# Eight heads of one attention item turned by VectorE and a DMA round trip instead of by TensorE

## Chip, cores and metric

One core of one Trainium2 chip runs the whole kernel. The metric is device microseconds of one execution; the kernel before took 1079.42 us (median of three runs: 1077.27, 1079.42, 1080.25).

## The reference, cut to what matters

All tensors are float32. There are 16 sequences of 128 tokens, width 512, 16 heads of 32 columns. The reference is a transformer layer followed by a second cross attention:

```
x  = x + attention(LN1(x) Wqkv) Wao            # stage A, mask_1x1xSxS2
x  = x + attention(LN2(x) Wq, ctx Wkv) Wco     # stage B, mask_Bx1xSxS2
x  = x + gelu(LN3(x) W1) W2                    # the MLP
x  = x + tanh(gate) * attention(x Wq', LNa(ctx) Wk', LNa(ctx) Wv') Wo'   # stage D, mask_BxS2
```

with, for each sequence and head,

```
P[q, k] = exp(scores[q, k] - max_k)      # scores = q k^T / sqrt(32), masked
out[q]  = (sum_k P[q, k] v[k]) / sum_k P[q, k]
```

TensorE contracts over the partitions. Softmax leaves the queries on the partitions of P, and the product with v needs the keys there, so each P (128 x 128, per head) has to be turned before the product.

## The kernel before

The attention stages are a software pipeline over 48 items: item g is sequence g % 16 of stage A (0 to 15), B (16 to 31) or D (32 to 47). Every engine has its own program, written out by hand in one order, and semaphores tie them together; there is no planner. `step` of each engine handles, in step g, the scores and softmax of item g, the turning and row sums of item g - 1, and the product with v, the context and the output projection of items g - 1 and g - 2 (`times_v(g - 2)`, `context(g - 2)`, `project_out(g - 2)`). Steps 46 and 47 of stage D stand in `last_steps_of_d`. Every projection is done as three products of split (hi, lo) parts.

A step also issues half units of the projections for the next pair of sequences on TensorE (L889, L897). Stage D has few of them left in its last steps: step 45 projects `units` 4 and 5 of the last pair.

There are three ways in which P is turned:

- By TensorE (`BY_PE`, L160): `exps` (L1397) writes the 16 heads to `prob`; `transpose_prob` (L919) turns them in four quarters of four heads (L935), two quarters at a time in banks 4 and 5 of PSUM; ScalarE copies quarters 0 and 2 back (`prob_out`, L1394), VectorE quarters 1 and 3 (L1850).
- Half and half (items neither in `BY_PE` nor in `WHOLE`): `exps` writes heads 0 to 7 to `prob_blocks` in an order of 32 x 32 blocks. VectorE transposes all the blocks in one instruction (`turn_blocks`, L1838 to L1841). Sync (the queue SP) stores the 512 KB to DRAM (`store_blocks`, L619 to L624), waits for the landing, and brings them back in four DMAs of 128 KB, each to 32 partitions of `prob` (`bring_blocks`, L626 to L633). TensorE turns only quarters 2 and 3, and ScalarE copies both in one instruction (`probs_out`, L1389; for item 43 as two of half the size, L1386).
- Whole (`WHOLE`, items 33 to 42): the second eight heads go the same way through `second_prob_blocks`.

`times_v(g)` (L968 to L994) waits for the copies and, for an exchanged item, for the four DMAs (`s_moved`, L979). The number of exchanges so far, the number of transposed quarters and of copies are derived from `BY_PE` by `moved_number`, `transposed_count`, `copied_by_act` and `copied_by_dve` (L167 to L194), so all waits follow the tuple.

The row sums of item g - 1 take their own way: `inverse_sums` on VectorE (L1835), a small transpose on TensorE (`row_sums`, L956), a copy by ScalarE (L1425), a store of 8 KB to DRAM (`store_row_sums`, L675) and four broadcast loads of 64 KB into `context` (`spread_row_sums`, L683), for which VectorE's `context` (L1856) waits.

Sync issues all DMAs in one order. In step 44 the last is (for an exchanged item) `store_blocks(44)`; in step 45 follow the mask of item 46, `store_stream(42)`, `bring_blocks(44)`, `store_row_sums(44)`, `spread_row_sums(44)`. Items 33 to 42 are whole, item 43 is half and half, items 44 to 47 are turned by TensorE. Step 45 has a special order on TensorE, since `sums_late(44)` (L450) is true: `times_v(43)`, `scores(45)`, both half units, `row_sums(44)`, two quarters of item 44, `project_out(43)` part 0, the other two quarters, part 1. The next instruction is `times_v(44)` (L1216).

Of the kernel before, what the change touches and what calls it, by code (L numbers as in the profile page):

```python
# [156 lines left out]

BY_PE = (0, 27, 28, 29, 30, 31, 44, 45, 46, 47)  # L160


WHOLE = tuple(range(33, 43))
# [3 lines left out]
def moved_number(g):  # L167

    return g + 1 - sum(k <= g for k in BY_PE)

# [6 lines left out]
def turned_by_pe(k):  # L177

    return 4 if k in BY_PE else 0 if k in WHOLE else 2


def transposed_count(g, c):

    return sum(turned_by_pe(k) for k in range(g)) + (c + 1 if g in BY_PE else c - 1)


def copied_by_act(g, half):

    return sum(turned_by_pe(k) // 2 for k in range(g)) + (half + 1 if g in BY_PE else 1)


def copied_by_dve(g, half):

    return sum(2 for k in range(g) if k in BY_PE) + (half + 1 if g in BY_PE else 0)  # L194

# [78 lines left out]
def build(nc, x, first_x, enc, encT, mask_a, mask_b, mask_d, weights, columns, rows, gate, ident_in, out):  # L274
# [3 lines left out]
    with ExitStack() as ctx:  # L278
# [160 lines left out]
        def item(st):  # L439

            return 16 * st.phase + st.b
# [4 lines left out]
        def value_bank(g, half):  # L446

            return T_BANK if g in WHOLE or g == 32 else T_BANK + half
# [62 lines left out]
        def sp_program():  # L511
# [114 lines left out]
            def bring_blocks(g):  # L626

                n = moved_number(g)
                sp.wait_ge(s_pst, 16 * n)
                blocks = turned[n % 2].rearrange("(i k) (j n) -> j k i n", i=4, j=4)  # L630
                for j in range(4):
                    dst = prob[32 * j:32 * j + 32, g % 2, 0:NH // 2 * T].rearrange("p (i n) -> p i n", i=4)
                    sp.dma_start(dst, blocks[j]).then_inc(s_moved, 16)  # L633

            def store_second_blocks(g):
                n = second_number(g)
                sp.wait_ge(s_turned2, n)
                if n > 2:
                    sp.wait_ge(s_moved2, 64 * (n - 2))
                sp.dma_start(turned_second[n % 2], second_blocks[:, :]).then_inc(s_pst2, 16)  # L640
# [67 lines left out]
            def step(st):  # L708
# [7 lines left out]
                if g - 1 in WHOLE:  # L716
                    store_second_blocks(g - 1)
                if st.prev and g - 1 not in BY_PE:
                    bring_blocks(g - 1)
# [1001 lines left out]
        def dve_program():  # L1721
# [67 lines left out]
            def make_mask_bias(g):  # L1789
                phase, b, par = g // 16, g % 16, g % 2  # L1790
                if phase == B:
                    dve.wait_ge(s_mask[par], 16 * (b // 2 + 1))
                    if b:
                        dve.wait_ge(s_biased, 2 * (g - 2) + 2 if b >= 2 else 32)
                    dve.tensor_scalar(mbias[:, par, :], msk[:, par, :], 1.0, 10000.0, ALU.subtract, ALU.mult).then_inc(s_mb, 1)
                if phase == D:
                    dve.wait_ge(s_mask[par], 16 * (8 + b // 2 + 1))
                    if b >= 2:
                        dve.wait_ge(s_masked, 2 * (g - 2) + 2)
                    dve.tensor_scalar(mbias[:, par, :], mrow[:, par, :], 1.0, 3e38, ALU.subtract, ALU.mult).then_inc(s_mb, 1)  # L1800
                    dve.wait_ge(s_mb, 16 + b + 1)
                    dve.tensor_scalar(mbias[:, par, :], mbias[:, par, :], 4.0, None, ALU.mult).then_inc(s_mb2, 1)
# [27 lines left out]
            def inverse_sums(g):  # L1830
                par = g % 2
                dve.wait_ge(s_exp, 4 * g + 4)
                if g >= 2:
                    dve.wait_ge(s_r, g - 1)
                dve.reciprocal(rtotal[:, par, :].rearrange("p (j c) -> p c j", c=KC),  # L1835
                               total[:, par, :].rearrange("p (c j) -> p c j", j=4)).then_inc(s_rt, 1)

            def turn_blocks(g):  # L1838

                dve.wait_ge(s_exp, 4 * g + 2)  # L1840
                dve.transpose(pblocks[:, :], pblocks[:, :]).then_inc(s_turned, 1)  # L1841

            def turn_second_blocks(g):

                dve.wait_ge(s_exp, 4 * g + 4)
                dve.transpose(second_blocks[:, :], second_blocks[:, :]).then_inc(s_turned2, 1)
# [5 lines left out]
            def context(g, h):  # L1852
                half = slice(256 * h, 256 * h + 256)
                dve.wait_ge(s_pv, 4 * g + (4 if value_bank(g, 1) == T_BANK else 2 * h + 2))
                dve.wait_ge(s_rsp, 64 * (g + 1))
                dve.tensor_tensor(ctxn[:, half], ps[:, value_bank(g, h), half], ctxn[:, half], ALU.mult).then_inc(s_cx, 1)  # L1856
# [80 lines left out]
            def step(st):  # L1937
                phase, b, g = st.phase, st.b, item(st)
                late = g == 2
                if g - 1 in WHOLE:  # L1940
                    inverse_sums(g - 1)
                    turn_second_blocks(g - 1)
                if g == 44:
                    inverse_sums(g - 1)
                    make_mask_bias(g)
                    mask_scores(g, 0)
                if st.ends and not late:
                    context(g - 2, 0)
                    context(g - 2, 1)
                if st.ends and not late and phase == D and g != 44:  # L1950
                    make_mask_bias(g)
                    mask_scores(g, 0)
                if st.ends and not late and g - 1 not in WHOLE and g != 44:
                    inverse_sums(g - 1)
                if st.ends and not late and g - 2 not in LO_BY_POOL:
                    context_lo(g - 2, 0)
                    context_lo(g - 2, 1)
                if not st.ends or late or phase != D:
                    make_mask_bias(g)
                    mask_scores(g, 0)  # L1960
                if late:
                    context(g - 2, 0)
                    context(g - 2, 1)
                if late and g - 1 not in WHOLE:
                    inverse_sums(g - 1)
                mask_scores(g, 1)
                if st.prev and not st.ends:
                    inverse_sums(g - 1)
                    row_max(g, 0)
                if g == 33:  # L1970
                    row_max(g, 1)
                if st.prev and g - 1 in BY_PE:
                    prob_out(g - 1, 1)
                v_out(*st.units[0])
                ahead_ln = st.ahead and st.ahead.ln is not None and st.ahead.kind == HERE
                later_ln = st.later and st.later.ln is not None and st.later != mlp_fill(0)
                if ahead_ln and later_ln:
                    normalise(st.ahead)
                if g == 28:
                    row_max(g, 0)  # L1980
                    prob_out(g - 1, 3)
                    turn_inputs(st.fill)
                    statistics(st.ahead)
                    row_max(g, 1)
                elif g == 29:
                    turn_inputs(st.fill)
                    row_max(g, 0)
                elif st.ends or not st.prev:
                    row_max(g, 0)
                    if st.fill in TURNED:  # L1990
                        turn_inputs(st.fill)
                if st.units[2]:
                    v_out(*st.units[1])
                if g == 1:
                    fill_hi(st.fill)
                    prob_out(0, 3)
                if g not in (28, 33):
                    row_max(g, 1)
                if late:
                    context_lo(g - 2, 0)  # L2000
                    context_lo(g - 2, 1)
                if g == 0:
                    turn_inputs(STEPS[A][1].fill)
                if st.prev and g - 1 in BY_PE and g not in (1, 28, 33):
                    prob_out(g - 1, 3)
                if ahead_ln and not later_ln and st.ahead != mlp_fill(0):
                    normalise(st.ahead)
                if g != 1 and st.fill and st.fill.ln is not None:
                    fill_hi(st.fill)
                if st.units[2]:  # L2010
                    v_out(*st.units[2])
                else:
                    v_out(*st.units[1])
                if st.ahead == mlp_fill(0):
                    normalise(st.ahead)
                if later_ln:
                    statistics(st.later)
                if g not in BY_PE:
                    turn_blocks(g)
                if st.ends:  # L2020
                    stream(g - 2)
# [155 lines left out]
            for p in range(5, NG * NPAIR):  # L2177
                g, jp = divmod(p, NPAIR)
# [266 lines left out]
```

## Time and profile before

| | us |
|---|---|
| median of the runs | 1079.42 |
| the profiled execution | 1078.77 |
| its span, first to last instruction | 1077.5 |
| TensorE busy | 1066.3 |
| VectorE busy | 816.7 |
| ScalarE busy | 704.0 |
| GpSimd busy | 465.4 |

Time stamps below are microseconds from the start of the span. TensorE's granted clock is 1.000 of full speed over the span. In rows, PE is TensorE, DVE VectorE, ACT ScalarE, POOL GpSimd, SPq the DMAs that Sync issues.

### The profile page before, as it was taken

To read this page: it belongs to the slowest core of one execution; us is meant where nothing else is said; L and a number is where in the kernel's file an instruction comes from. 1 tells how busy PE (TensorE), PEld (TensorE's weight loads), DVE (VectorE), ACT (ScalarE), POOL (GpSimd) and SP (SyncE) were. 2 spreads that over 40 slices of the span, in tenths; PEclk is the share of its full clock that TensorE was granted. 3 is DMA by queue.
4 is the path that set the end of the run, shared out by engine and by line. 5 is a ranking of instruction groups with operands and counts; after the bars stand their busy time and mean duration, and the time that the engine had idled before them with its cause. 6 is when DMAs were issued, how large, how long until landed. Compare 5 with 4: busy or idle time off the path is not lost.

```text
span 1077.5 us, 24230 instructions
## 1 busy us (share of the span) xinstructions
PE 1066.3 (99%) x8741; PEld 924.5 (86%) x8741; DVE 816.7 (76%) x1315; ACT 704.0 (65%) x2355; POOL 465.4 (43%) x349
## 2 busy tenths in 40 slices
PE   8999999999999999999999999999999999999998
PEld 7989888888888888887898888888888998888886
DVE  7778887777888888888978667767697467777677
ACT  5777787777778888797444544544455276666676
POOL 4676565576777776763213122114032233333220
DMA  7356666577767777555153152351647636777621
GB/s 250 109 188 210 197 211 185 184 207 225 218 217 224 228 212 234 184 182 163 67 156 110 56 168 64 113 155 42 215 137 266 224 124 207 222 210 206 200 72 61
DMA packets 145928, 185.93 MB, mean 173 GB/s; under 512 B 17952, under 2 KB 88848, under 8 KB 145808
## 3 DMA queue, kind: packets, MB, share of 16 engines
q1 hardware_dynamic: 145808, 184.37, 54.8%
q8 instruction: 70, 1.15, 0.5%
q14 instruction: 50, 0.41, 0.1%
HBM read 122.59 MB, written 61.73 MB: 171 GB/s over the span
## 4 chain that ended last, share of the span: by engine, by line
PE 83%; DVE 6%; ACT 4%; DMA 2%; POOL 2%; issue 2%; SPq 0%; DVEq 0%; ACTq 0%; POOLq 0%
PE psum L897 23%; PE psum L1101 15%; PE psum L1080 15%; PE psum L889 10%; PE psum L1016 9%; PE psum L915 4%; PE psum L993 3%; PE psum L935 3%; ACT prob_blocks L1416 1%; ACT prob L1416 1%; POOL inputs_lo L2269 1%; ACT inputs_transposed L1454 1%; DMA inputs_transposed<-encT_in 1%; POOL prob L2283 1%; DVE weights_lo L1726 1%
## 5 line engine op out<-in xcount | busy, mean ns | idle before, releaser
L897 PE MATMUL psum<-inputs_hi,weights_hi 128*128 128x256 f32 x768 | 224.4, 292 | 0.8 <-POOL inputs_lo L2269 0.4
L897 PE MATMUL psum<-inputs_lo,weights_hi 128*128 128x256 f32 x768 | 217.1, 283 | 0.0
L897 PE MATMUL psum<-inputs_hi,weights_lo 128*128 128x256 f32 x768 | 216.9, 282 | 0.0
L2283 POOL TENSOR_TENSOR prob<-prob,mask_bias 128x1024 f32<-128x1024 f32 x64 | 152.6, 2406 | 92.5 <-DVE prob L1814 92.0
L897 PEld LDWEIGHTS psum<-inputs_hi,weights_hi 128*128 128x128 f32 x768 | 146.6, 191 | 7.7 <-issue 1.7
L1827 DVE TENSOR_REDUCE negmax<-prob 128x8 f32<-128x1024 f32 x96 | 115.8, 1212 | 48.5 <-POOL prob L2283 48.4
L2269 POOL TENSOR_TENSOR inputs_lo<-inputs_transposed,inputs_hi 128x512 fp32r<-128x512 f32 x70 | 93.7, 1359 | 129.7 <-DVE inputs_hi L1787 98.2
L1416 ACT ACTIVATE prob<-prob,negmax 128x128 f32<-128x128 f32 x384 | 148.3, 392 | 0.6 <-DVE negmax L1827 0.5
L897 PEld LDWEIGHTS psum<-inputs_lo,weights_hi 128*128 128x128 f32 x768 | 146.9, 191 | 0.2
L897 PEld LDWEIGHTS psum<-inputs_hi,weights_lo 128*128 128x128 f32 x768 | 146.9, 191 | 0.0
L1416 ACT ACTIVATE prob_blocks<-prob,negmax 128x128 f32<-128x128 f32 x304 | 117.8, 391 | 19.8 <-DVE negmax L1827 19.7
L1016 PE MATMUL psum<-weights_hi,context_parts 128*128 128x512 f32 x376 | 126.0, 394 | 1.1 <-ACT qT L1362 0.4
L1503 ACT ACTIVATE qT<-psum,columns 128x512 f32<-128x512 f32 (+1 forms) x80 | 46.2, 598 | 98.8 <-PE psum L1080 98.8
L2286 POOL TENSOR_TENSOR residual<-residual,bias_rows 128x512 f32<-128x512 f32 x42 | 58.1, 1389 | 70.0 <-DMA residual<-stream 50.2
L1101 PE MATMUL psum<-weights_hi,hidden_parts 128*128 128x512 f32 x264 | 87.6, 392 | 0.3
L1016 PEld LDWEIGHTS psum<-weights_hi,context_parts 128*128 128x128 f32 x376 | 70.6, 188 | 17.4 <-issue 0.8
L1916 DVE SCALAR_TENSOR_TENSOR kT<-kT,qT 128x512 f32<-128x512 f32 x64 | 46.1, 721 | 50.4 <-ACT kT L1508 50.2
L1101 PE MATMUL psum<-weights_hi,context_parts 128*128 128x512 f32 x248 | 81.6, 390 | 0.7 <-DVE context_parts L1911 0.7
L1814 DVE SCALAR_TENSOR_TENSOR prob<-psum,mask 128x512 f32<-128x512 f32 x128 | 79.2, 680 | 3.2 <-ACT gate L1681 3.2
L1454 ACT ACTIVATE inputs_transposed<-inputs_transposed,columns 128x256 f32<-128x256 f32 x120 | 62.3, 590 | 26.8 <-DVE inputs_transposed L1756 26.8
L1080 PE MATMUL psum<-hidden_inputs,weights_hi 128*128 128x512 f32 x256 | 78.9, 389 | 0.0
L889 PE MATMUL psum<-weights_hi,inputs_hi 128*128 128x512 f32 x184 | 75.2, 409 | 0.2 <-ACT v L1373 0.2
(138 smaller groups left out, 2638.2 us busy)
## 6 DMA issues: line engine op xcount, KB each, us to landing
weights_whole<-weights_in SPq DMA_DIRECT2D x80, 256.0 KB, 3.4
prob_turned<-prob_blocks SPq DMA_DIRECT2D x38, 512.0 KB, 3.0
prob<-prob_turned SPq DMA_DIRECT2D x152, 128.0 KB, 3.4
inputs_transposed<-normalised SPq DMA_DIRECT2D x120, 128.0 KB, 2.8
normalised<-ln_tile SPq DMA_DIRECT2D x24, 512.0 KB, 2.8
context<-row_sums_spread SPq DMA_DIRECT2D x188, 64.0 KB, 2.0
stream<-residual SPq DMA_DIRECT2D x42, 256.0 KB, 3.1
ln_tile<-stream SPq DMA_DIRECT2D x32, 256.0 KB, 3.5
```

Source lines behind the costliest of these rows:

```text
L889: mm = pe.matmul(ps[:, bank, :], a[:, buf, c, tok], w[:, slot, c, :], start=c == 0 and i == 0, stop=c == KC - 1 and i == 2)
L897: mm = pe.matmul(ps[:, bank, GT * part:GT * part + GT], w[:, slot, c, o], a[:, buf, c, :], start=c == 0 and i == 0, stop=c == KC - 1 and i ...
L1016: mm = pe.matmul(ps[:, U_BANK + 1, :], a[0][:, cs], w[:, slot, c, :], start=c == 0 and i == 0, stop=c == KC - 1 and i == 2)
L1080: mm = pe.matmul(out, w[:, slot, c, o], a, start=c == 0 and i == 0, stop=c == KC - 1 and i == 2)
L1101: mm = pe.matmul(ps[:, accumulator(group, t), :], a[gb][:, tok], w[:, slot, (j * chunks + e) % 4, :], start=j == 0 and e == 0 and i == 0, ...
L1416: ins = act.activation(dst, src, ACT.Exp, bias=negmax[:, par, s:s + 1], accum_out=total[:, par, s:s + 1])
L1454: ins = act.activation(dst, src, ACT.Identity, bias=cols[:, b0 + c:b0 + c + 1], scale=cols[:, g0 + c:g0 + c + 1])
L1814: ins = dve.scalar_tensor_tensor(heads(P[:, 512 * c:512 * c + 512]), ps[:, S_BANK:S_BANK + 4, T * c:T * c + T], SCALE, other.unsqueeze(1). ...
L1827: dve.tensor_reduce(negmax[:, par, 8 * h:8 * h + 8], heads(prob[:, par, 1024 * h:1024 * h + 1024]), AX.X, ALU.max, negate=True).then_inc(s ...
L2269: pool.tensor_tensor(lo, y, hi.bitcast(f32), ALU.subtract).then_inc(s_rlo if fill.ln is None else s_flo, 1)
L2283: pool.tensor_tensor(half, half, mb.unsqueeze(1).to_broadcast([128, 8, T]), ALU.add).then_inc(s_biased, 1)
L2286: pool.tensor_tensor(tile, tile, brow[:, ROW_SLOT[name], :], ALU.add).then_inc(s_resb, 1)
```

## The change

Item 44 leaves `BY_PE`, so it is exchanged half and half like item 43. The general place of `turn_blocks(g)` is the end of VectorE's step g; for item 44 it is put into step 45 instead, between `context(43)` and the mask and scores of item 45.

```diff
-BY_PE = (0, 27, 28, 29, 30, 31, 44, 45, 46, 47)
+BY_PE = (0, 27, 28, 29, 30, 31, 45, 46, 47)
...
                 if st.ends and not late:
                     context(g - 2, 0)
                     context(g - 2, 1)
+                if g == 45:
+                    turn_blocks(44)
                 if st.ends and not late and phase == D and g != 44:
                     make_mask_bias(g)
                     mask_scores(g, 0)
...
-                if g not in BY_PE:
+                if g not in BY_PE and g != 44:
                     turn_blocks(g)
```

By the derived conditions, for item 44: `exps` writes quarters 0 and 1 to `prob_blocks`; TensorE's `transpose_prob(44, 0)` and `(44, 1)` are gone, and quarters 2 and 3 come before `project_out(43)` part 0; VectorE's two copies (L1850) are gone, and ScalarE's two (L1394) become one of twice the size (L1389); Sync issues one store and four loads more.

## Rows read from the trace of the kernel before

**Rows 1.** The page, busy time, share of the span and instructions of each engine.
```profile
PE 1066.3 (99%) x8741; PEld 924.5 (86%) x8741; DVE 816.7 (76%) x1315; ACT 704.0 (65%) x2355; POOL 465.4 (43%) x349
```

**Rows 2.** Windows, step 45 of TensorE: busy by engine, PEclk, DMA share, GB/s.
```profile
1030.41:1043.33 12.92, 12.92 (x142) 11.55 (x141) 8.10 (x14) 9.19 (x42) 2.55 (x3) 1.00 0.17 52
```

**Rows 3.** The chain that ended last: start, us, what.
```profile
1027.47 3.01 PE psum L1016 x12
...
1038.65 0.87 PE psum L935 x8
...
1041.14 0.87 PE psum L935 x8
...
1043.40 1.01 PE psum L993 x32
...
1048.90 0.11 PE psum L956
...
1063.26 0.74 DVE weights_whole L1883
```

**Rows 4.** Timeline of VectorE: start, us, instruction, idle before and its releaser.
```profile
1017.27 1.25 DVE L1841 STREAM_TRANSPOSE prob_blocks<-prob_blocks 128x1024 f32<-128x1024 f32 x1 [2.54 <-ACT prob_blocks L1416]
...
1031.67 0.76 DVE L1856 TENSOR_TENSOR context<-psum,context 128x256 f32<-128x256 f32 x2 [0.41 <-DMA context<-row_sums_spread]
1032.35 0.22 DVE L1800 TENSOR_SCALAR mask_bias<-mask_rows 128x128 f32<-128x128 uint8 x1
...
1032.96 1.29 DVE L1814 SCALAR_TENSOR_TENSOR prob<-psum,mask_bias 128x512 f32<-128x512 f32 x2
1035.61 0.26 DVE L1835 RECIPROCAL rtotal<-total 128x16 f32<-128x16 f32 x1 [1.36 <-ACT prob L1416]
...
1044.11 0.80 DVE L1856 TENSOR_TENSOR context<-psum,context 128x256 f32<-128x256 f32 x2
...
1045.07 0.23 DVE L1802 TENSOR_SCALAR mask_bias<-mask_bias 128x128 f32<-128x128 f32 x1
1045.58 1.29 DVE L1814 SCALAR_TENSOR_TENSOR prob<-psum,mask_bias 128x512 f32<-128x512 f32 x2 [0.28 <-PE psum L915]
1046.91 1.22 DVE L1827 TENSOR_REDUCE negmax<-prob 128x8 f32<-128x1024 f32 x1
```

**Rows 5.** Timeline of ScalarE.
```profile
1016.75 0.40 ACT L1416 ACTIVATE prob_blocks<-prob,negmax 128x128 f32<-128x128 f32 x1
...
1027.31 1.08 ACT L1386 ACTIVATE prob<-psum 128x512 f32<-128x512 f32 x2
...
1031.99 0.40 ACT L1416 ACTIVATE prob<-prob,negmax 128x128 f32<-128x128 f32 x1
...
1042.11 0.39 ACT L1416 ACTIVATE prob<-prob,negmax 128x128 f32<-128x128 f32 x1
```

**Rows 6.** Timeline of Sync's DMA issues: start, time that the issues took.
```profile
196.83 0.34 SPq L624 DMA_DIRECT2D prob_turned<-prob_blocks  x1
...
199.50 1.75 SPq L633 DMA_DIRECT2D prob<-prob_turned  x4
...
1025.46 0.48 SPq L675 DMA_DIRECT2D row_sums_spread<-row_sums_transposed  x1
1028.36 1.71 SPq L683 DMA_DIRECT2D context<-row_sums_spread  x4
...
1038.98 0.32 SPq L675 DMA_DIRECT2D row_sums_spread<-row_sums_transposed  x1
1040.38 1.71 SPq L683 DMA_DIRECT2D context<-row_sums_spread  x4
```

**Rows 7.** DMA issues from 1000 to 1060: count, KB, median us to landing.
```profile
prob<-prob_turned SPq DMA_DIRECT2D x8, 128.0 KB, 3.0
```

**Rows 8.** Landing of all stores (L624), first line, and all loads (L633), second.
```profile
DMA to landing us min/median/max: 2.6/3.0/4.8
...
DMA to landing us min/median/max: 2.4/3.4/5.6
```

## The prediction

> **What bounds the kernel now.** I read the page's busy times first. TensorE is busy 1066.3 of 1077.5 us [rows 1], so a change pays only as far as it lets TensorE pass on sooner. The window of the changed step says the same locally: TensorE is busy for all of its 12.92 us at full granted clock, VectorE for 8.10 and ScalarE for 9.19, and the DMA engines are at 0.17 [rows 2]. Then the chain in order of time. From 1027.47 up to the output projection before 1063.2 it runs on TensorE without a wait, then it changes to VectorE [rows 3]. In it stand eight transposes of item 44 at 1038.65 and eight more at 1041.14, 0.87 us each group, and `times_v(44)` at 1043.40. Last I read the timelines of the other engines around the step, since what TensorE gives up must be ready elsewhere by an earlier time than now.
>
> **The change part by part.** The sum is made against the profiled execution (1078.77 us, span 1077.5); the median shown is 0.65 us above it, and that difference is put back at the end.
>
> *Removed on TensorE.* Quarters 2 and 3 now take the first place, so the second group of eight goes: 0.87 us. The rest of the step keeps its times: the half units before are untouched, and twelve products of the projection took 3.01 us where nothing was between them [rows 3]. From the first product of `project_out(43)` (the end of the first group, 1038.65 + 0.87 = 1039.52) to `times_v(44)` it was 3.88 us, and becomes 3.01. So 0.87 us at most, and `times_v(44)` is wanted at 1042.53.
>
> The Trainium skill ("TensorE: Matmul & The Clock Gate", Part 4: PE-mode transpose) puts a 128x128 transpose at about 275 ns within a kernel; by that the eight would be 2.2 us, an estimate. The trace has a duration for the same thing, 0.87 / 8 = 0.11 us, and that is used.
>
> *Added on VectorE.* One block transpose of 1.25 us. In item 43 it started 0.52 us after the start of the eighth exponential (1017.27 against 1016.75, [rows 4, 5]). The eighth of item 44 starts at 1031.99 [rows 5], so the transpose starts at about 1032.51, 0.16 us after the point where the mask bias now starts (1032.35), and ends at 1033.76. The mask bias to the first masked scores were 0.61 us (1032.35 to 1032.96) and the scores 1.29 [rows 4]. So they end at 1033.7 + 0.6 + 1.3 = 1035.6. VectorE there sat idle for 1.36 us until 1035.61, when ScalarE was through with item 44 [rows 4]. That idle time is the cover, and it is used up almost to the end; were it gone, the row sums of item 44, which TensorE takes only at 1038.54, still have over 2 us. I cost the transpose at 0. The two copies leave VectorE. ScalarE waits for the first group of transposes only (end 1039.52) and makes two quarters' copies in one, 1.08 us as in item 43; so it can start the exponentials of item 45 at about 1040.7 and not at 1042.11 [rows 5]. ScalarE is not on the chain, so this too is 0.
>
> *The exchange.* Sync's `store_blocks(44)` now holds everything behind it until 1033.8: the mask of item 46 and the store of stream 42, which nobody wants before 1044. Store to first load took 2.67 us where nothing else was in the way (196.83 to 199.50), the four loads took 1.75 us to issue [rows 6]. So the loads go out from 1036.5 to 1038.2, the last issued at about 1037.8, and with 3.0 us to landing [rows 7] `prob` is complete at 1040.8. The wait in `times_v(44)` looks for it at 1042.53: 1.7 us to spare, 0 cost. From the other end: with the longest landings of the run, 4.8 for the store and 5.6 for a load [rows 8], it is 1033.8 + 4.8 + 1.3 + 5.6 = 1045.5, TensorE would stand 3.0 us and the kernel lose 2.1. At a DMA share of 0.17 [rows 2] I take the near end.
>
> *The row sums behind the exchange.* This is what I expect to be late next. TensorE's order gives the row sums of item 44 at the same time as now, and Sync issues their store at 1038.98 [rows 6]; it is then free, by 0.8 us. But four loads of 128 KB have just been issued ahead. Store to first broadcast took 1.40 us here, with nothing ahead, and 2.90 us in step 44, right behind the exchange of item 43 (1025.46 to 1028.36). Those are the bounds. The case lies between, as the store is issued some 0.8 us after the last load and there is no stream store in between: I take 2.0. From the first broadcast to `context` took 3.31 us where VectorE waited for it (1028.36 to 1031.67) [rows 4, 6]. So `context(44)` can start at T = 1038.98 + 2.0 + 3.3 = 1044.3, bounds 1043.7 and 1045.2; now it is 1044.11. The Trainium skill ("DMA: Bandwidth & Descriptors", Queues, rings and completion order) says that each DMA engine consumes one ring's descriptors in order; by that the 8 KB wait for all of what was issued before them. The two rows, 1.40 and 2.90, are in line with it.
>
> What follows T on VectorE: mask bias done at T + 1.19 (1045.30 against 1044.11), masked scores to row maximum 1.33 (1045.58 to 1046.91), row maximum 1.22, then the inverse sums of item 45, 0.26 as for item 44, in all T + 4.0 [rows 4]. TensorE takes the row sums of item 45 at 1048.90 in the chain, 1048.03 after a full gain. With 0.1 us for the hand over (my allowance), T up to 1043.95 costs nothing and each microsecond beyond costs one. T = 1044.3 costs 0.35. The lower bound costs 0, the upper 1.25.
>
> **Sum:** -0.87 + 0.35 = -0.5 us. TensorE's later waits in steps 46 and 47 are for products that move along with it, and VectorE's part of the chain from 1063.26 is released by TensorE [rows 3]; ScalarE, earlier by 1.4 us, does not hold it. So the half microsecond reaches the end: 1078.3 for an execution like the profiled one, 1079.42 - 0.5 = 1078.9 as a median.
>
> **The rivals.**
>
> *All of it (15%).* The row sums pass the loads unhindered, T is 1043.7: -0.87 us, 1078.55. For it: Sync issues them late enough that the loads may be in their landing phase. Against it: the 1.5 us that item 43's cost.
>
> *Row sums fully held (17%).* T = 1045.2, cost 1.25, sum +0.4: 1079.8. It decides against the change from T = 1044.8, where the wait of row sums 45 eats the 0.87. For it, the 2.90 of [rows 6]; against it, that one had a stream store and the loads directly ahead.
>
> *The exchange lands late (9%).* This is the slower side in earnest: `times_v(44)` waits for the loads, everything on TensorE behind it shifts. It decides from a landing at 1043.4 (1042.53 + 0.87). At the longest landings it is +2.1 us, 1081.5. Against it, 1.7 us of room and quiet DMA engines.
>
> *ScalarE was the hidden bound (6%).* Then its 1.4 us come through: 1078.0. Against it, the chain without a ScalarE piece in these steps.
>
> *The transposes are worth what the page says (2%).* If the modelled ends hide time and each really holds TensorE 2.5 times as long as the pitch in [rows 3], the removal gives 2.2 us: 1077.2 with nothing lost behind. That is the rule cited above; the pitch of 0.11 in this trace speaks against.
>
> *The change does not do what it says (2%):* a wait in another place keeps the old times: 1079.4.
>
> **How the numbers follow.** The forecast, between -0.2 and -0.8 us, has 45%, the rivals 51% as given, and 4% are left for what I do not see. A difference of 0.3%, 3.2 us, is about what a measurement of this kernel can tell from no change, since three runs already lie 3 us apart. No case above reaches it by its own price; the scatter between executions and the unseen 4% give the tails. So 6% faster, 88% within, 6% slower. The range for the time is set by that scatter around the cases: the cases of most weight run from 1078.0 to 1079.8, the two outer runs lie 2.15 below and 0.83 above the median, so 1076.7 to 1081.0.
>
> **What would show it.** Eight L935 instead of sixteen between 1038 and 1043, and `times_v(44)` (L993) at 1042.5 without a wait for a DMA; if a wait `prob<-prob_turned` stands there, the exchange was late. One L1841 at 1032.5, with the reciprocal at 1035.6 as before. The first L683 of item 44 at 1041.0 (1040.4 and 1041.9 are the rivals), `context(44)` on VectorE behind an idle time put to the broadcast at 1044.3. A wait of about 0.3 us of TensorE at L956 of item 45. ScalarE's exponentials of item 45 from 1040.7. The prediction is wrong if the time moves by more than 3 us, or if the step shortens by something other than one group of eight transposes.

## The result, and the profile after

The changed kernel took 1081.07 us (median of 11 runs, 1078.51 to 1083.12) against 1078.49 us for the one before (11 runs, 1077.27 to 1080.25): a ratio of 1.002, 95% interval 1.0012 to 1.0028. It is slower by 1.3 to 3.0 us, which the interval tells from no change, though it is less than the 0.3% that the prediction named. A second comparison gave 1.0028 (1.0019 to 1.0038). The prediction said 1078.9 and a gain of half a microsecond. It started from a median of three runs, 1079.42, which eleven runs put at 1078.49; against that, half a microsecond would have been 1078.0.

| | before | after |
|---|---|---|
| span of the profiled execution | 1077.5 | 1079.8 |
| `times_v(43)` on TensorE | 1030.41 | 1030.87 |
| from there to `times_v(44)` | 12.92 | 12.02 |
| from there to the end of the span | 47.09 | 48.93 |

The two profiles are 0.46 us apart before the change begins, so all stamps below are best read from `times_v(43)`. Behind it the changed kernel is slower by 1.84 us.

First, TensorE in the changed step (timeline; start, us, idle before). There is one group of eight transposes between `times_v(43)` and `times_v(44)`, and `times_v(44)` waits for nothing. The time went at the row sums of item 45 (L956), 8.3 us later.

```profile
1038.95 1.03 PE L935 MATMUL psum<-identity,prob 128*128 128x128 f32 x8
...
1042.89 1.08 PE L993 MATMUL psum<-prob,v 128*32 128x128 f32 x32
...
1051.21 0.28 PE L956 MATMUL psum<-identity,rtotal 128*16 128x128 f32 x1 [2.72 <-DVE rtotal L1835]
```

A wait of 2.72 us less the 0.90 won before it is 1.82, the whole of the 1.84. What the wait hangs on is in the chain that ended last (start, us, what). It leaves TensorE at the row sums of item 44 and comes back 12 us later; in the chain before [rows 3] it never left it here.

```profile
1039.00 0.12 PE psum L956
...
1039.15 0.28 ACT row_sums_transposed L1425
...
1039.44 2.60 DMA row_sums_spread<-row_sums_transposed
...
1042.06 0.31 SPq L683
...
1043.35 3.73 DMA context<-row_sums_spread
...
1048.09 0.24 DVE mask_bias L1802
...
1049.06 0.69 DVE prob L1814
...
1050.91 0.26 DVE rtotal L1835
...
1051.21 0.28 PE psum L956
```

VectorE (timeline). The block transpose waited 0.24 us for ScalarE and started where it was predicted (1032.51, and 0.46 for the shift). The inverse sums of item 44 (L1835) stand where they stood from `times_v(43)` (5.20 us behind it in both kernels, [rows 4]); `context(44)` waited 3.42 us for the broadcast.

```profile
1032.98 1.25 DVE L1841 STREAM_TRANSPOSE prob_blocks<-prob_blocks 128x1024 f32<-128x1024 f32 x1 [0.24 <-ACT prob_blocks L1416]
...
1036.07 0.26 DVE L1835 RECIPROCAL rtotal<-total 128x16 f32<-128x16 f32 x1
...
1047.17 0.76 DVE L1856 TENSOR_TENSOR context<-psum,context 128x256 f32<-128x256 f32 x2 [3.42 <-DMA context<-row_sums_spread]
```

Sync (timeline of the issues, beside [rows 6]). The row sums are stored at the same place as before, but behind four loads, and 2.62 us lie between that store and the first broadcast instead of 1.40.

```profile
1034.25 0.34 SPq L624 DMA_DIRECT2D prob_turned<-prob_blocks  x1
...
1037.01 1.75 SPq L633 DMA_DIRECT2D prob<-prob_turned  x4
1039.44 0.31 SPq L675 DMA_DIRECT2D row_sums_spread<-row_sums_transposed  x1
1042.06 1.71 SPq L683 DMA_DIRECT2D context<-row_sums_spread  x4
```

From the first broadcast to `context` it took 5.11 us, and I had read 3.31. The semaphore events of the trace say more: the four broadcasts give 64 increments. 63 had come by 1045.28, the last at 1047.08, 1.8 us behind. The trace does not say from which DMA engine it came. One thing stands in the trace at that time, a fetch of 16 KB of instructions (kind "instruction", here in the DMA view of 1045.00 to 1045.25: packets, MB, share of 16 engines; it ended at 1046.03).

```profile
q8 instruction: 1, 0.02, 24.0%
```

The queue q8 brought 1.15 MB in 70 such fetches in the profile's page of before. The Trainium skill ("Runtime: NRT & Kernel Launch", Instruction fetch mechanics) says that instructions come in blocks of 16 KiB, 256 of them, over the sequencer's own DMA queue, and calls the cost "mostly hidden". The packets agree with the 16 KB. By the page's figure 70 fetches are some 17,900 instructions, an estimate; TensorE's products and weight loads are 17,482 [rows 1], so I take the fetches for TensorE's. That their cost was hidden here is what the experiments call into doubt.

### The profile page after: what moved, and what is told of

The parts are those of the page before. It is cut to its first block, busy times and chain, and to the rows that moved or that the text cites. A ratio compares the mean times of both kernels' runs of the same rounds, so it can differ in the third digit from the quotient of the medians.

```text
span 1079.8 us, 24216 instructions
## 1 busy us (share of the span) xinstructions
PE 1066.0 (99%) x8733; PEld 924.4 (86%) x8733; DVE 816.9 (76%) x1314; ACT 704.1 (65%) x2354; POOL 465.4 (43%) x349
## 3 DMA queue, kind: packets, MB, share of 16 engines
q8 instruction: 70, 1.15, 0.5%
## 4 chain that ended last, share of the span: by engine, by line
PE 82%; DVE 5%; ACT 4%; DMA 3%; POOL 2%; issue 2%; SPq 1%; DVEq 0%; ACTq 0%; POOLq 0%
PE psum L897 23%; PE psum L1101 15%; PE psum L1080 15%; PE psum L1016 9%; PE psum L889 9%; PE psum L915 4%; PE psum L993 3%; PE psum L935 3%; ACT prob_blocks L1416 1%; POOL prob L2285 1%; ACT prob L1416 1%; POOL inputs_lo L2271 1%; DMA context<-row_sums_spread 1%; DMA row_sums_spread<-row_sums_transposed 1%; DVE weights_lo L1726 1%
## 5 line engine op out<-in xcount | busy, mean ns | idle before, releaser
L1416 ACT ACTIVATE prob<-prob,negmax 128x128 f32<-128x128 f32 x376 | 145.1, 391 | 1.3 <-DVE negmax L1827 1.3
L1416 ACT ACTIVATE prob_blocks<-prob,negmax 128x128 f32<-128x128 f32 x312 | 120.9, 391 | 20.2 <-DVE negmax L1827 19.7
L1016 PE MATMUL psum<-weights_hi,context_parts 128*128 128x512 f32 x376 | 125.7, 394 | 1.0 <-DVE context_parts L1862 0.5
L1016 PEld LDWEIGHTS psum<-weights_hi,context_parts 128*128 128x128 f32 x376 | 70.7, 188 | 17.3 <-DVE context_parts L1862 0.9
```

The costliest lines, as they stand in the source:

```text
L1016: mm = pe.matmul(ps[:, U_BANK + 1, :], a[0][:, cs], w[:, slot, c, :], start=c == 0 and i == 0, stop=c == KC - 1 and i == 2)
L1416: ins = act.activation(dst, src, ACT.Exp, bias=negmax[:, par, s:s + 1], accum_out=total[:, par, s:s + 1])
```

## The experiments

Theory A: the exchange's DMAs delay the round trip of item 44's row sums, and `context(44)`, the scores of item 46 and the inverse sums of item 45 pass that on to TensorE. Theory B: the moved transposes and copies cost. Theory C: VectorE's order costs. Theory F (from the fetch above): the late increment is late because of an instruction fetch. The table has, from each profile, the stretch from `times_v(43)` to the end ("rest"), the start of the first broadcast, the last increment of the broadcasts and the end of the fetch, all from `times_v(43)`, and TensorE's wait at L956 of item 45. Each row is one profile; where TensorE has no wait to explain (before, e2, e7, e8), the rest lies between 46.84 and 47.09, so a difference of 0.2 us in it is nothing.

| kernel | ratio to before (95%) | rest | first broadcast | last increment | fetch ends | wait |
|---|---|---|---|---|---|---|
| before | | 47.09 | 9.97 | 13.25 | 15.56 | 0 |
| changed | 1.0020 (1.0012 to 1.0028) | 48.93 | 11.19 | 16.21 | 15.16 | 2.72 |
| changed, again | 1.0028 (1.0019 to 1.0038) | 49.05 | 11.27 | 16.37 | 15.19 | 2.85 |
| e1_traffic | 1.0006 (0.9997 to 1.0015) | 47.74 | 11.63 | 14.99 | 15.71 | 0.64 |
| e2_turn | 0.9999 (0.9990 to 1.0008) | 46.86 | 9.97 | 13.28 | 16.01 | 0 |
| e3_stream_later | 1.0024 (1.0013 to 1.0035) | 48.91 | 11.64 | 16.22 | 14.84 | 2.72 |
| e4_sums_first | 0.9988 (0.9979 to 0.9997) | 45.94 | 9.44 | 12.94 | 15.62 | 0 |
| e4_again | 0.9996 (0.9986 to 1.0006) | 46.05 | 9.44 | 12.83 | 15.46 | 0 |
| e5_sums_pe | 1.0030 (1.0018 to 1.0042) | 48.30 | 11.13 | 15.63 | 14.44 | 2.28 |
| e6_fetch | 1.0012 (1.0003 to 1.0020) | 47.77 | 11.36 | 14.65 | 16.55 | 1.15 |
| e7_fetch_before | 1.0010 (1.0001 to 1.0019) | 47.01 | 9.97 | 13.23 | 16.83 | 0 |
| e8_sums_before | 0.9998 (0.9989 to 1.0006) | 46.84 | 8.52 | 11.81 | 15.51 | 0 |
| e9_act_queue | 1.0003 (0.9994 to 1.0012) | 47.55 | 11.42 | 14.81 | 15.79 | 0.69 |
| e10_fetch_earlier | 1.0054 (1.0039 to 1.0069) | 50.48 | 11.07 | 16.15 | 14.97 | 2.65 |
| e11_traffic_fetch | 1.0021 (1.0007 to 1.0035) | 47.66 | 11.74 | 14.99 | 15.64 | 0.63 |
| e12_fetch_later | 1.0015 (1.0004 to 1.0026) | 47.16 | 11.19 | 14.49 | 16.33 | 0.99 |

The ratio holds the whole kernel, the rest only what lies behind the start of the changed step. The kernels that change the start (e6, e7, e10, e11, e12) also move what is ahead of it: in e10 and e11 `times_v(43)` comes at 1032.52 and 1036.14, 1.7 and 5.3 us later than in the changed kernel, and only the start of e6 has a control (e7). So for these the rest, the increments and the wait are what counts, and the whole times of e10, e11 and e12 are not taken apart here.

**e1_traffic**: the exchange's DMAs, TensorE as before. VectorE's block transpose of e2 (below) is in it too, since the store waits for it.

```diff
+                if g == 44:                                    # Sync, step 44
+                    sp.wait_ge(s_turned2, 11)
+                    sp.dma_start(turned_second[1], second_blocks[:, :]).then_inc(s_pst2, 16)
...
+                if g == 45:                                    # Sync, ahead of store_row_sums(44)
+                    sp.wait_ge(s_pst2, 16 * 11)
+                    blocks = turned_second[1].rearrange("(i k) (j n) -> j k i n", i=4, j=4)
+                    for j in range(4):
+                        dst = second_blocks[32 * j:32 * j + 32, :].rearrange("p (i n) -> p i n", i=4)
+                        sp.dma_start(dst, blocks[j]).then_inc(s_moved2, 16)
```

> The kernel before, with TensorE still turning item 44, plus a block transpose on VectorE in step 45 and an exchange of the same size at the same places of Sync's order (512 KB store, four loads of 128 KB, into a tile that nobody reads). Theory A (the exchange's DMAs make the round trip of the row sums of item 44 late, and that time is passed on by context(44), the masked scores of item 46 and the inverse sums of item 45 to TensorE): context(44) starts at about 1047 instead of 1044.1, TensorE waits at L956 of item 45 some 1.8 us (2.7 in the changed kernel less the 0.87 that it had gained), the kernel is slower than before by the same 2.2 us as the changed one, as the end hangs on the landing and not on TensorE. Theory B (the loss comes from what moved on the engines: the order of the transposes and copies on TensorE and ScalarE): no loss, within 0.3 us of before.

Its chain, and its longest wait of TensorE:

```profile
1039.53 3.04 DMA row_sums_spread<-row_sums_transposed
...
1043.87 2.08 DMA context<-row_sums_spread
```
```profile
PE psum L966 <- DVE rtotal L1845: 0.6, 1, 0.6
```

The traffic alone makes TensorE wait where the changed kernel waits (L966 here is L956 there), so B falls as the whole cause. But it is 0.6 us and not 1.8: the store took even longer (3.04), and the last broadcast did not (2.08). A is right in kind. Of the 1.84 us lost it gives a third; of the 2.96 us by which the last increment is late in the changed kernel (16.21 against 13.25) it gives 1.74, since the first part of any lateness is covered before TensorE waits.

**e2_turn**: the block transpose alone, without a DMA.

```diff
+                if g == 45:
+                    dve.wait_ge(s_pst2, 16 * second_number(42))
+                    dve.wait_ge(s_exp, 4 * 44 + 2)
+                    dve.transpose(second_blocks[:, :], second_blocks[:, :]).then_inc(s_turned2, 1)
```

> The kernel before plus only the block transpose on VectorE between context(43) and the mask of item 45 (on a tile that nobody reads), no DMA. Theory A: it lies in VectorE's idle 1.36 us, the inverse sums of item 44 stay where they were to 0.1 us, no change of the time (within 0.3 us). Rival C (VectorE's order is what costs, since the masked scores of item 45 come 1.2 us later): the loss of about 2 us is here already.

Ratio 0.9999, no wait: C is out, and the transpose costs nothing, as predicted.

**e3_stream_later**: the 256 KB store that follows the broadcasts goes behind those of item 45.

```diff
-                if st.ends and g not in (2, 34):
+                if st.ends and g not in (2, 34, 46):
                     store_stream(g - 3)
...
                     spread_row_sums(g - 1)
+                if g == 46:
+                    store_stream(43)
```

> The changed kernel, with the store of stream 43 (256 KB) issued behind the broadcasts of item 45 instead of 0.5 us behind those of item 44. Theory A2 (the store of the stream shares the DMA engines with the broadcasts and makes the last one land after 3.7 us instead of 2.0): the last broadcast lands in 2.0 us, context(44) starts 1.7 us earlier than in the changed kernel, TensorE's wait at L956 falls from 2.7 to about 1.0, the time is 1.7 us under the changed kernel, +0.5 against before. Rival A1 (the loads of the exchange, still under way, are what the broadcasts wait for): no change against the changed kernel, the landing stays at 3.7 us.

A miss: 48.91 against 48.93. Two of the 64 increments come 1.0 and 1.2 us behind the others with no store there. The stream's store is not what holds them.

**e4_sums_first**: the changed kernel, with the row sums ahead of the loads on both engines.

```diff
-                    project(*st.units[1], U_BANK + 1)
+                    if g == 45:
+                        project(*st.units[1], U_BANK + 1, (0,))
+                        row_sums(g - 1)
+                        project(*st.units[1], U_BANK + 1, (1,))
...
+                if g == 45:
+                    store_row_sums(g - 1)
                 if st.prev and g - 1 not in BY_PE:
                     bring_blocks(g - 1)
-                if st.prev:
+                if st.prev and g != 45:
                     store_row_sums(g - 1)
```

> The changed kernel, with the row sums of item 44 taken by TensorE between the two parts of the second half unit (1.5 us earlier) and their store issued by Sync ahead of the four loads of the exchange. Theory A: the 8 KB land in about 1.4 us, the broadcasts go out from about 1040.5 behind the loads, context(44) starts by 1044.5, TensorE waits for nothing at L956 of item 45; the 0.87 us of the removed transposes are kept: 0.9 us faster than before, if the loads, now 0.5 us later, still land before TensorE wants them. Theory B: as slow as the changed kernel, +2.2.

The store goes out 7.14 us behind `times_v(43)` instead of 8.57, and 2.30 us lie between it and the first broadcast, most of it Sync's issuing of the loads. Its chain runs on TensorE without a break from `times_v(43)` to item 46's projection:

```profile
1030.53 1.01 PE psum L995 x32
...
1037.16 0.11 PE psum L958
1037.27 1.43 PE psum L899 x12
1038.70 0.87 PE psum L937 x8
1039.57 2.84 PE psum L1018 x12
1042.45 1.08 PE psum L995 x32
...
1048.02 0.11 PE psum L958
```

The rest is 45.94 us, 1.15 under before and 0.90 under e8 and e2: the 0.9 of the transposes reach the end once the row sums are in time. The loads were waited for by nobody, so the exchange itself is not what is late.

**e5_sums_pe**: only TensorE's half of that edit.

> The changed kernel with only the TensorE half of the last version: row sums of item 44 taken 1.5 us earlier, while Sync still stores them behind the four loads. Theory A (ring order behind the loads is what costs): Sync is free at 1038.8 only, the store stands right behind the loads and lands after about 2.9 us, so context(44) starts no more than 0.5 us earlier than in the changed kernel; about +1.5 to +2.2 us against before. Rival D (it was the time at which TensorE gives the sums): it is as fast as e4_sums_first, -1.

In step 45 it is as theory A has it: the store stands 8.07 us behind `times_v(43)`, right behind the loads, and lands after 3.04 us; the wait is 2.28. The whole time misses the expectation: 1083.07 is 3.7 us above before, and in the rest it loses only 1.2. In its profile `times_v(43)` comes at 1033.90, 3.0 us later than in the changed kernel. That time went in pieces of under 1 us over the items from 1 to 32, all ahead of the edit; why is not shown.

**e8_sums_before** and **e4_again**: the control for the gain, in one comparison. e8 is the kernel before with TensorE's half of the edit.

> The kernel before (item 44 turned by TensorE) with only the row sums of item 44 taken 1.5 us earlier by TensorE, as in e4_sums_first. Control: if e4_sums_first gains because the removed transposes are now kept as a gain, this is unchanged against before (within 0.3 us), since context(44) starts at 1044.11 behind stream(43) and not behind the broadcasts. If it gains 1 us too, the earlier row sums are what helps, and the exchange gives nothing.

> The changed kernel with row sums of item 44 earlier and their store ahead of the loads, once more, on the chip of the control: 1 us faster than before (0.9 from the transposes), TensorE without a wait from times_v(43) to the projection of item 46, times_v(44) some 12.0 us behind times_v(43) instead of 12.9.

The early row sums alone give nothing (0.9998). e4 gave 0.9996 this time and 0.9988 the first. In this comparison its median is 1078.08 against 1078.87 for e8 and 1079.04 for before; the second interval includes 1. In both profiles the rest is 1.0 to 1.15 us below before. Against the controls in which nothing waits (46.84 to 47.09) it is 0.8 to 1.15. So a version that beats the changed kernel clearly and the one before by about 0.9 us exists, though the runs settle the latter only by half.

**e6_fetch** and its control **e7_fetch_before**: TensorE's stream shortened at the very start.

```diff
-            for k in range(10):
+            for k in range(2):
                 pe.matmul(ps[:, U_BANK + 1, 0:128], zeros, zeros, start=True, stop=True)
```

> The changed kernel with 8 of the 10 products of zeros at the kernel's very start left out, 32 instructions of TensorE fewer; nothing near item 44 is touched. In the changed kernel a 16 KB instruction fetch (DMA queue q8) begins at 1045.05, while the last broadcast of item 44's row sums is under way, and that broadcast takes 3.73 us to land instead of 2.0; in the one with the dummy exchange the fetch began at 1045.3 with the broadcasts' packets through, and it took 2.08. Theory F (the DMA engine that brings TensorE's instructions does so ahead of its share of the broadcast): the fetch moves 32 TensorE instructions later, to 1047 or 1048, the last broadcast lands in 2.0 to 2.1 us, TensorE's wait at L956 of item 45 falls from 2.7 to about 1.0, the time falls by 1.7 us to within 0.5 of before. Rival G (the broadcasts are slow for another reason, TensorE's or ScalarE's traffic in SBUF at that time): the landing stays above 3 us wherever the fetch is.

> The kernel before with the same 8 products of zeros left out: the control for e6_fetch. No change is expected (within 0.4 us) by either theory, unless the start itself needs them; what it shows is to be taken off e6_fetch's time.

e6's chain:

```profile
1041.00 2.77 DMA row_sums_spread<-row_sums_transposed
...
1045.08 2.00 DMA context<-row_sums_spread
```

No increment is late, the wait is 1.15 us, the rest 1.2 us shorter than in the changed kernel. The row sums' store is as slow as there (2.77), so the two effects come apart: about 1 us of wait stays with the loads, the rest went with the fetch. The medians say the same. Beside before at 1079.34, the changed kernel took 1082.15, e6 1080.43 and e7 1080.08. e7 missed its expectation of no change: the shorter start itself costs about 0.7. Taking that off, e6 is 0.35 us above its control where the changed kernel is 2.8 above its own. So without the fetch's share the change is about even, and no gain: the wait that the loads cause eats the 0.9.

**after_again**:

> The changed kernel once more, on the chip of this comparison. Expected 2.2 us above before, with the fetch again between 1044.8 and 1045.4 and the last broadcast landing after 3 us or more; if the fetch falls behind the broadcasts' last packet in this execution, theory F expects 2.1 us and a shorter wait.

The same again: one increment 1.8 us behind the others, wait 2.85. The fetch began at 1045.56, a little past the stretch that was named, and still fell on the last broadcast.

**e9_act_queue**: the row sums' store on ScalarE's own queue.

```diff
-                if st.prev:                                    # Sync
+                if st.prev and g != 45:
                     store_row_sums(g - 1)
...
+                if g == 45:                                    # ScalarE
+                    act.wait_ge(s_rc, g)
+                    act.wait_ge(s_rsp, 64 * (g - 1))
+                    act.dma_start(spread.rearrange("j (c n) -> (j c) n", c=KC), rsumT[:, :]).then_inc(s_rst, 16)
```

> The changed kernel with the 8 KB store of item 44's row sums issued by ScalarE on its own queue, right behind the copy; the loads stay where they are on Sync's queue. Theory H (the store waits because it stands behind the loads in the same ring of each DMA engine): in another ring it lands after about 1.4 to 1.7 us instead of 2.6 to 3.0, the broadcasts go out a microsecond earlier and end before the instruction fetch, so the last lands in 2.0 to 2.2 us, context(44) starts about 2 us earlier than in the changed kernel, TensorE's wait at L956 is 0.3 to 1.0 us. Rival I (the engines are busy with the loads whatever the ring): the landing stays at 2.6 us or more, and nothing changes.

```profile
1038.53 2.83 DMA row_sums_spread<-row_sums_transposed
...
1042.66 2.10 DMA context<-row_sums_spread
```

Theory H falls: with nothing ahead of it in its own queue the store still takes 2.83 us. What it follows can be read from the landings. In all ten profiles with the loads ahead of it, this one with its other queue included, the store lands 0.17 or 0.18 us behind the last of the four loads (here 11.40 against 11.23 us behind `times_v(43)`). In e5 it is issued 0.5 us earlier and gains nothing by it. The same holds throughout the kernel: over all sixteen traces a row sums' store that was issued while loads of an exchange were under way landed 0.15 to 0.35 us behind the last of them in 592 of 618 cases, and never before it.

The section that I cited for the ring order (the Trainium skill, "DMA: Bandwidth & Descriptors", Queues, rings and completion order) says two things on this. An engine takes its queues in turn, which alone would let the small store pass early. But a semaphore increment lands only after every earlier write of its engine, across the queues; the 0.17 us agree with this one. Another queue is no way round.

No increment was late here, and the kernel was on a par with before (1.0003). The edit has a price of its own: ScalarE's issue stands ahead of its copy of `qT`, for which TensorE waits 0.57 us at L1016.

**e10_fetch_earlier, e11_traffic_fetch, e12_fetch_later**: 16, 14 and 6 products of zeros instead of 10, in the changed kernel, in e1 and in the changed kernel.

> The changed kernel with 16 instead of 10 products of zeros at the start: 24 TensorE instructions more, so the fetch near item 44 comes a few tenths of a microsecond earlier than in the changed kernel (about 13.7 us behind times_v(43) instead of 14.2). Theory F (a fetch that an engine starts on while the last broadcasts are being issued holds that engine's share back): it still falls on the broadcasts, one or two of the 64 increments come 1.3 to 1.8 us late, TensorE waits 2.5 to 3 us at L956. Rival G (chance, or something else in the changed kernel): no relation to the place of the fetch.

> The dummy exchange of e1_traffic (TensorE still turns item 44) with 14 instead of 10 products of zeros: the fetch comes some tenths earlier than in e1_traffic, where it began 14.36 us behind times_v(43), just too late to hold the last broadcast (2.08 us to landing). Theory F: now it holds it, the last broadcast lands after 3.3 us or more, TensorE's wait at L956 of item 45 rises from 0.6 to about 1.9 us. Rival G: 2.1 us and 0.6 us as in e1_traffic.

> The changed kernel with 6 instead of 10 products of zeros: 16 TensorE instructions fewer, the fetch 1 to 2 us later than in the changed kernel, behind the broadcasts. Theory F: the last broadcast lands in 2.0 to 2.2 us, TensorE waits about 1 us at L956, as in e6_fetch. Rival G: as slow as the changed kernel (3.7 us, 2.7 us).

e10 and e12 came out as theory F says (late, not late). e11 did not test it: its fetch began 14.50 us behind `times_v(43)`, not earlier than in e1 (14.36) but later, and it repeated e1, with a fetch under way and nothing late. Over all kernels with the loads ahead of the row sums: the increments were late in the five whose fetch ended by 15.2 us (changed, changed again, e3, e5, e10), and on time in the two whose fetch came later altogether (e6, e12) and in the three whose fetch ended at 15.6 to 15.8 (e1, e11, e9). In these last three the fetch itself took 1.14 to 1.50 us, in the changed kernel 0.96 and 0.88 (but in e3 1.28). In the five, the late increment came 1.0 to 1.4 us behind the fetch's end: in e5 the fetch ended 0.7 us earlier than in the changed kernel, and the increment came 0.6 us earlier. That looks like one engine serving the fetch and its share of the broadcast one behind the other, either first. It is a reading of ten profiles, made after them, and the traces do not name the engine.

Rival G, chance, can be tested on the other items. Each trace has 47 such groups of four broadcasts, 752 in all. In 41 the last increment came over 0.8 us behind the last but two. Of the 123 groups with a fetch under way in the 2.0 us behind the issue of the fourth broadcast it was so in 37, of the 629 without one in 4. Leaving item 44 out, it is 32 of 115 against 4 of 621. So the fetch is what holds the increment, and e6 and e12, which touch nothing else near item 44, show it for this item; but most fetches hold nothing, and the exact condition is open.

The profile of e10 shows a second price. Its rest is 1.5 us longer than the changed kernel's at the same wait. The windows say why (busy by engine, granted clock, DMA share, GB/s):

```profile
1049.00:1052.00 3.00, 1.17 (x8) 0.74 (x6) 2.80 (x7) 0.75 (x2) 0.00 (x0) 1.00 0.00 0
1052.00:1055.00 3.00, 2.19 (x11) 1.72 (x12) 2.78 (x7) 1.88 (x9) 0.00 (x0) 0.91 0.01 3
1055.00:1058.00 3.00, 3.00 (x13) 2.64 (x12) 1.13 (x3) 1.93 (x9) 0.00 (x0) 0.53 0.33 87
1058.00:1061.00 3.00, 3.00 (x69) 2.27 (x67) 2.83 (x7) 2.91 (x14) 0.00 (x0) 1.00 0.00 0
```

TensorE had stood for 2.65 us and had started again at 1052.81. At 1054.4 its granted clock fell from 2.4 to 1.2 GHz, for 3.4 us, in which eight transposes took 1.71 us instead of 0.87:

```profile
1053.54 2.04 PE psum L1016 x6
1055.59 1.71 PE psum L935 x8
1057.29 1.70 PE psum L1016 x6
```

The profile of the changed kernel has no such fall after the same wait. The profile of e11 has one elsewhere: TensorE stood for 1.76 us until 302.16, and the clock fell at 303.7, again for 3.4 us. For the other runs the mean granted clock is on record, which does not say where it fell. It was below 1 in 20 of the 36 runs of the five kernels with a wait of 2.28 us or more (changed, changed again, e3, e5, e10), in 4 of 53 of those with 0.6 to 1.2 us (e1, e6, e9, e11, e12), in 1 of 53 with none (e2, e4, e4 again, e7, e8) and in 3 of 102 of before. In the first 11 runs of the changed kernel, the six with the lower clock have a median of 1081.73 us and the five at full clock 1079.90. It does not account for e10's time: its three runs at full mean clock took 1084.95 to 1086.07, more than the profiled one with the fall (1084.29).

## Why the prediction was wrong, point by point

*Removed on TensorE, 0.87 us: right.* `times_v(43)` to `times_v(44)` fell by 0.90.

*Added on VectorE, 0 us: right*, in the profile (inverse sums of item 44 unmoved) and by e2. ScalarE's earlier exponentials (1040.94 in the changed kernel) were worth nothing, as said.

*The exchange, 0 us for the loads themselves: right.* `times_v(44)` did not wait, the loads went out 2.76 us behind the store of the blocks (2.67 predicted). The last of them landed 3.55 us after its issue where I took the median of 3.0, 0.6 us later than predicted; TensorE did not need it by then, but the row sums' store did. The rival of the late exchange, which held the slower side of my forecast, did not occur.

*The row sums behind the exchange, T = 1044.3 with bounds of 1043.7 and 1045.2: this step failed, in size and in its upper bound.* It was named as what would be late next, with the right place on TensorE. Measured from the same start, T was 47.17 - 0.46 = 1046.7. The 2.4 us have two parts. Store to first broadcast was 2.62 us where I took 2.0, inside the bounds of 1.40 and 2.90: 0.6 us. It is the 0.6 us of the last load, since the store lands right behind it. My 2.0 was a guess between two rows; it fits the median landing of a load, but I did not have that rule. First broadcast to `context` was 5.11 where I took 3.31 from one row and gave no bounds: 1.8 us, the fetch's share. The trace of before had them: among the figures I put on record is a load that landed after 5.6 us with a median of 3.4 [rows 8], and I took such a spread for the exchange's DMAs alone. The broadcasts' own spread stands there too (L683 in the kernel before):

```profile
DMA to landing us min/median/max: 1.8/2.0/3.5
```

Two of its 47 groups, items 29 and 36, have an increment held back like that of item 44 here, with a fetch under way. With 1.5 us more for this term the upper bound of T would have been 1046.7. A term with a DMA in it that is released by the last of 64 increments needed an upper end like this.

*From T to TensorE, one for one from 1043.95: right.* With T = 1046.71 it gives a wait of 2.76; measured 2.72. In e1, where TensorE gains nothing and the threshold is 0.87 later, T = 1046.05 less 0.55 gives 0.68; measured 0.64.

*The sum.* Left out altogether was that a wait of TensorE of nearly 3 us can cost more in clock, 1.5 us in the profile of e10. I had looked at the clock in the window of the changed step in the kernel before [rows 2], where TensorE never stands. With 0.87 - 2.76 the model gives +1.9 us; the median moved by 2.6, in line with a clock that falls in part of the runs: the five at full clock have a median 1.4 us above before, the six others 3.2. That this is the whole of the 0.7 is not shown.

*The range.* It does not follow from what it is said to follow from: the cases from 1078.0 to 1079.8, widened by 2.15 below and 0.83 above, give 1075.9 to 1080.6 and not 1076.7 to 1081.0. That the measured 1081.07 comes so near its upper end is luck: the median it starts from was 0.9 us too high.

The rival "row sums fully held" was the nearest in kind, and at +0.4 us it had the price of its landing bound. A loss should have had far more weight: T above 1044.8 turns the sign, 0.5 us above my value, where the first part alone had 0.9 us of room upward and the second another 1.5.

## What to carry to other kernels

Work taken off the engine that bounds the kernel is only won if the next thing that it waits for comes earlier by as much; here that was a chain of two small DMAs, and the DMAs which replaced the work were put right ahead of it. Issue the small latency-bound transfer first and the big one behind it, as e4 does: that order, not another queue, kept the gain. Bound a DMA landing by the spread of its kind over the trace and not by one quiet row, and allow for what a wait of some microseconds can cost in granted clock when the engine starts again.

## What the runs showed of the hardware

An 8 KB store took 1.40 us to its dependent issue with no loads ahead and 2.5 to 3.2 us behind four loads of 128 KB, from the same queue as from another (2.83); it landed 0.17 us behind the last of the loads, whichever queue it came from. Four broadcasts of 64 KB give 64 increments, and the one that waits for them waits for the last: one came 1.8 us late, and taking 16 or 32 instructions out of the beginning of TensorE's program, a millisecond earlier, removed that. Over all traces such a late increment stood in 37 of 123 groups with an instruction fetch under way and in 4 of 629 without. TensorE's granted clock fell to half 1.6 us after the end of a wait of 2.65 us, for 3.4 us; whether it fell varied from run to run of one kernel.
